# Two-layer decoder: one transposing transfer per causal query tile, weight loads in mid unit, fourth tile finished in its own slot

## The reference

```
# layer 0                                   # layer 1
q, k = rope(x @ Wq), rope(x @ Wk)           q, k = x @ W_Q, x @ W_K      # no rope
v = x @ Wv                                  v = x @ W_V
s = q @ k.T / sqrt(128); s[causal] = -inf   the same
y = softmax(s) @ v ; y @ Wo                 the same
x = layernorm(x + y)
```

## Time and profile before

| | |
|---|---|
| runs of the kernel before | 2684.7 us median, 2680.32 to 2685.36 |
| profiled execution, whole | 2686.01 us |
| its span | 2684.1 us, granted TensorE clock 0.964 on average |
| PE busy | 2436.8 us, 91% of the span |
| DVE, ACT | 1852.3 us (69%), 1587.0 us (59%) |
| POOL | 715.6 us (27%) |

### The profile page before, as it was taken

One profiled execution on the slowest core, in us unless ns is written; L12 is line 12 of the kernel. 1 busy time (PEld: TensorE's weight loads), 2 busy tenths in 40 slices (PEclk: granted clock), 3 DMA queues, 4 the chain that ended last, 5 costly groups with the idle time before them and its releaser, 6 DMA issues. The chain is left out here.

```text
span 2684.1 us, 58413 instructions
## 1 busy us (share of the span) xinstructions
PE 2436.8 (91%) x21345; PEld 1575.8 (59%) x21584; DVE 1852.3 (69%) x3371; ACT 1587.0 (59%) x2718; POOL 715.6 (27%) x671
## 2 busy tenths in 40 slices
PE   6988997989999999999678999998899999999964
PEld 4555664546666666665355666665466666665432
DVE  4776676657777777775556666667478888885597
ACT  4767665158877778874134555554167777774243
POOL 5565656601111011112233222215300000012211
PEclk8999999999999999999888999999899999999987
DMA  3333335325666666666240334435167777776400
GB/s 91 87 75 84 85 73 106 118 48 108 114 116 116 109 111 116 114 112 131 106 165 3 97 86 90 92 84 136 36 123 144 145 145 145 148 150 131 108 0 32
DMA packets 777604, 273.63 MB, mean 102 GB/s; under 512 B 746097, under 2 KB 748913, under 8 KB 775793
## 3 DMA queue, kind: packets, MB, share of 16 engines
q1 hardware_dynamic: 775696, 265.85, 47.0%
q0 software_dynamic: 1760, 5.77, 0.9%
HBM read 84.55 MB, written 6.44 MB: 34 GB/s over the span
## 5 line engine op out<-in xcount | busy, mean ns | idle before, releaser
L846 ACT ACTIVATE ph<-p,ri 128x1024 bf16<-128x1024 f32 (+4 forms) x512 | 437.4, 854 | 455.7 <-DVE ri L1155 367.7
L1165 DVE SCALAR_TENSOR_TENSOR pl<-p,ri,ph 128x1024 bf16<-128x1024 f32 (+4 forms) x512 | 510.5, 997 | 141.0 <-issue 71.7
L1225 PE MATMUL ps<-wo_hi,v_hi 128*128 128x128 bf16 x2688 | 479.2, 220 | 65.8 <-DMA wo_lo<-pl 65.2
L1227 PE MATMUL ps<-wo_hi,v_lo 128*128 128x128 bf16 x2688 | 478.9, 220 | 0.0
L1226 PE MATMUL ps<-wo_lo,v_hi 128*128 128x128 bf16 x2688 | 478.8, 220 | 0.0
L857 ACT ACTIVATE p<-p,nb 128x1024 f32<-128x1024 f32 (+4 forms) x512 | 435.5, 851 | 49.6 <-DVE nb L1148 36.3
L1225 PEld LDWEIGHTS ps<-wo_hi,v_hi 128*128 128x128 bf16 x2688 | 263.6, 98 | 139.4 <-DMA wo_lo<-pl 91.0
L1226 PEld LDWEIGHTS ps<-wo_lo,v_hi 128*128 128x128 bf16 x2688 | 263.9, 98 | 37.4
L1226 PE MATMUL ps<-k_lo,q_hi 128*128 128x512 bf16 (+2 forms) x767 | 271.5, 354 | 7.1 <-issue 0.4
L1227 PE MATMUL ps<-k_hi,q_lo 128*128 128x512 bf16 (+3 forms) x768 | 271.7, 354 | 0.1
L1227 PEld LDWEIGHTS ps<-wo_hi,v_lo 128*128 128x128 bf16 x2688 | 264.1, 98 | 0.0
(11 more groups left out here) (191 smaller groups left out, 5668.9 us busy)
## 6 DMA issues: line engine op xcount, KB each, us to landing
raw_kv<-in_wkvself SPq DMA_DIRECT2D x32, 512.0 KB, 3.6
raw_q<-in_wqself SPq DMA_DIRECT2D x32, 256.0 KB, 2.7
wo_hi<-ph SPq DMA_TRANSPOSE x512, 3.2
wo_lo<-pl SPq DMA_TRANSPOSE x512, 3.1
raw_q<-in_woself SPq DMA_DIRECT2D x32, 256.0 KB, 3.0
raw_q<-in_wqcross SPq DMA_DIRECT2D x32, 256.0 KB, 2.9
raw_q<-in_wocross SPq DMA_DIRECT2D x32, 256.0 KB, 3.0
raw_kv<-in_wkvcross SPq DMA_DIRECT2D x24, 256.0 KB, 3.1
```

What stands on the lines that cost most here:

```text
L846: nc.scalar.activation(m["ph"][:, qt % 2, 0:w], m["p"][:, qt % 2, 0:w], ACT.Copy, scale=ri[:, qt % 2:qt % 2 + 1]).then_inc(p_norm, 1)
L1165: nc.vector.scalar_tensor_tensor(out=m["pl"][:, qt % 2, 0:w], in0=m["p"][:, qt % 2, 0:w], scalar=ri[:, qt % 2:qt % 2 + 1], in1=m["ph"][:, ...
L1225: nc.tensor.matmul(o, l(0), r(0), start=first, stop=False)
L1227: return nc.tensor.matmul(o, l(1), r(0), start=False, stop=last)
```

## The change

1. In causal layers `ph` and `pl` of one tile lie side by side in one tile `phl`, and one transposing transfer moves both, when the remainder is done. SP issues 4 instead of 8 per unit, of 2, 4, 6 and 8 blocks of 128x128. `tr_in` counts 16 for a tile in place of 32 (`landed`).
2. In causal layers the weight loads are issued in the middle of units with n % 4 = 0 and 2, between the transfers of tiles 0 and 1, in place of the start of units 1 and 2.
3. In self0 the split of raw_kv moves from slot 1 to slot 0, that of raw_q from slot 2 to slot 1, and slot 0's rope comes behind the kv split on POOL.
4. In self1 the fourth tile is finished in its own slot on ACT and DVE. Nothing of it is left for the next unit.
5. `units` runs 4 units apart, 6 x 4 in a loop, 4 apart, in all looped stages.

```diff
@@ split_plan
-                first = 1 if self.rope else 2
+                first = 0 if self.rope else 2
@@ units
-            unit(0, None)
-            with engine.Fori(0, 7) as it:
+            for n in range(4):
+                unit(n, None)
+            with engine.Fori(0, 6) as it:
                 for i in range(4):
-                    unit(1 + i, it)
-            for n in range(UNITS - 3, UNITS):
+                    unit(4 + i, it)
+            for n in range(UNITS - 4, UNITS):
                 unit(n, None)
@@ SP, transposed and unit
+                    if L.causal:
+                        sp.wait_ge(p_lo, at(count, n, it))
+                        sp.nop(nofuse=True)
+                        sp.dma_start_transpose(m["pT"][qt][:, 0:2 * w // P, :], m["phl"][:, qt % 2, 0:2 * w]).then_inc(tr_in[qt], 16)
+                        return
...
-                    if n % 4 in (1, 2) and n // 4 < H // 2 - 1:
-                        j = n % 4 - 1
...
+                    loading = n % 4 in ((0, 2) if L.causal else (1, 2)) and n // 4 < H // 2 - 1
...
                             transposed(*((n, it, qt - 1) if qt else (n - 1, it, QT - 1)))
+                        if loading and L.causal and qt == 1:
+                            next_pair()
@@ POOL, unit
-                        if L.rope:
+                        if L.rope and qt:
                             rope(n, it, qt, L.jobs(n, qt))
...
+                        if L.rope and qt == 0:
+                            rope(n, it, qt, L.jobs(n, qt))
@@ ACT, unit
-                        if n or qt:
+                        if qt or n and not (L.causal and not L.rope):
                             rounded(*((n, it, qt - 1) if qt else (n - 1, it, QT - 1)))
...
+                        if (L.causal and not L.rope) and qt == QT - 1:
+                            rounded(n, it, qt)
                         job_parts(n, it, qt, L.jobs(n, qt))
@@ DVE, unit
-                        if n or qt:
+                        pending = qt or n and not (L.causal and not L.rope)
+                        if pending:
                             inverse(*prior)
                         scores(n, it, qt)
                         job_parts(n, it, qt, L.jobs(n, qt), ("QN",))
-                        if n or qt:
+                        if pending:
                             remainder(*prior)
+                        if (L.causal and not L.rope) and qt == QT - 1:
+                            inverse(n, it, qt)
+                            remainder(n, it, qt)
```

More of the change, by code:

```diff
@@ L217, in build, with landed @@
             c["ln"] += NT
+        def landed(L, n):
+            return c_tr[L.name] + (16 if L.causal else 32) * (n + 1)
+        c_tr = dict(self0=0, cross0=16 * UNITS, self1=48 * UNITS, cross1=64 * UNITS)
         def units(engine, unit, L):
@@ L302, in build @@
                 m["any"] = sb("any", [P, B], F32, s)
-            m["ph"] = sb(f"ph{li}", [P, 2, L.kv], BF16, s)
-            m["pl"] = sb(f"pl{li}", [P, 2, L.kv], BF16, s)
+            both = sb(f"phl{li}", [P, 4, L.kv], BF16, s)
+            if L.causal:
+                m["phl"] = both[:, :, :].rearrange("p (s k) n -> p s (k n)", s=2)
+                m["ph"] = lambda qt, w, q=m["phl"]: q[:, qt % 2, 0:w]
+                m["pl"] = lambda qt, w, q=m["phl"]: q[:, qt % 2, w:2 * w]
+            else:
+                m["ph"] = lambda qt, w, q=both: q[:, qt % 2, 0:w]
+                m["pl"] = lambda qt, w, q=both: q[:, 2 + qt % 2, 0:w]
             m["wo"] = [sb(f"wo{li}_{k}", [P, H, D], BF16, s) for k in hl]
             tail = [t[:, H // 2:, :].rearrange("p h n -> p (h n)") for t in m["wo"]]
-            m["pT"] = [t[:, 0:QT * L.kt * P].rearrange("p (i k q) -> p i k q", i=QT, k=L.kt) for t in tail]
+            if L.causal:
+                pairs = [t[:, 0:QT * L.kt * P].rearrange("p (i k q) -> p i k q", i=2, k=2 * L.kt) for t in tail]
+                m["pT"] = [pairs[i // 2][:, i % 2, :, :] for i in range(QT)]
+            else:
+                m["pT"] = [t[:, 0:QT * L.kt * P].rearrange("p (i k q) -> p i k q", i=QT, k=L.kt) for t in tail]
             if L.causal:
@@ L441, in transposed, with next_pair @@
                         sp.nop(nofuse=True)
+                    if L.causal:
+                        sp.wait_ge(p_lo, at(count, n, it))
+                        sp.nop(nofuse=True)
+                        sp.dma_start_transpose(m["pT"][qt][:, 0:2 * w // P, :], m["phl"][:, qt % 2, 0:2 * w]).then_inc(tr_in[qt], 16)
+                        return
                     sp.wait_ge(p_norm, at(count, n, it))
                     sp.nop(nofuse=True)
[L444 removed]
+                    sp.dma_start_transpose(m["pT"][0][:, qt, 0:w // P, :], m["ph"](qt, w)).then_inc(tr_in[qt], 16)
                     sp.wait_ge(p_lo, at(count, n, it))
                     sp.nop(nofuse=True)
[L447 removed]
+                    sp.dma_start_transpose(m["pT"][1][:, qt, 0:w // P, :], m["pl"](qt, w)).then_inc(tr_in[qt], 16)
                 def unit(n, it):
[L450 to L451 removed]
+                    def next_pair():
+                        j = n % 4 // 2 if L.causal else n % 4 - 1
                         sp.wait_ge(w_split, at(lambda n: base + 2 * (n // 4) + j + 1, n, it))
[L453 to L454 removed]
+                        qkv(at(lambda n: n // 4 + 1, n, it), j, None)
+                    loading = n % 4 in ((0, 2) if L.causal else (1, 2)) and n // 4 < H // 2 - 1
+                    if loading and not L.causal:
+                        next_pair()
                     if n == UNITS - 3:
@@ L843, in rounded @@
                     if bn >= 0:
-                        act.wait_ge(tr_in[bq], at(lambda n: 32 * (c["u"] + behind(n, qt, 2)[0] + 1), n, it))
+                        act.wait_ge(tr_in[bq], at(lambda n: landed(L, behind(n, qt, 2)[0]), n, it))
                     act.wait_ge(r_inv, at(lambda n: c["s"] + QT * n + qt + 1, n, it))
-                    nc.scalar.activation(m["ph"][:, qt % 2, 0:w], m["p"][:, qt % 2, 0:w], ACT.Copy, scale=ri[:, qt % 2:qt % 2 + 1]).then_inc(p_norm, 1)
+                    nc.scalar.activation(m["ph"](qt, w), m["p"][:, qt % 2, 0:w], ACT.Copy, scale=ri[:, qt % 2:qt % 2 + 1]).then_inc(p_norm, 1)
                 def unit(n, it):
                     for qt in range(QT):
-                        if n or qt:
+                        if qt or n and not (L.causal and not L.rope):
                             rounded(*((n, it, qt - 1) if qt else (n - 1, it, QT - 1)))
@@ L879, in _ @@
                 units(act, unit, L)
-                rounded(UNITS - 1, None, QT - 1)
+                if not (L.causal and not L.rope):
+                    rounded(UNITS - 1, None, QT - 1)
                 if L.name in EARLY:
@@ L1161, in remainder @@
                     if bn >= 0:
-                        dve.wait_ge(tr_in[bq], at(lambda n: 32 * (c["u"] + behind(n, qt, 2)[0] + 1), n, it))
+                        dve.wait_ge(tr_in[bq], at(lambda n: landed(L, behind(n, qt, 2)[0]), n, it))
                     dve.wait_ge(p_norm, at(lambda n: c["s"] + QT * n + qt + 1, n, it))
                     dve.nop(nofuse=True)
-                    nc.vector.scalar_tensor_tensor(out=m["pl"][:, qt % 2, 0:w], in0=m["p"][:, qt % 2, 0:w], scalar=ri[:, qt % 2:qt % 2 + 1],
-                                                   in1=m["ph"][:, qt % 2, 0:w], op0=ALU.mult, op1=ALU.subtract).then_inc(p_lo, 1)
+                    nc.vector.scalar_tensor_tensor(out=m["pl"](qt, w), in0=m["p"][:, qt % 2, 0:w], scalar=ri[:, qt % 2:qt % 2 + 1],
+                                                   in1=m["ph"](qt, w), op0=ALU.mult, op1=ALU.subtract).then_inc(p_lo, 1)
                 def unit(n, it):
@@ L1199, in _ @@
                 units(dve, unit, L)
-                inverse(UNITS - 1, None, QT - 1)
-                remainder(UNITS - 1, None, QT - 1)
+                if not (L.causal and not L.rope):
+                    inverse(UNITS - 1, None, QT - 1)
+                    remainder(UNITS - 1, None, QT - 1)
                 quantise_run(EARLY.get(L.name, ()))
```

5 lines of the change are left out of this document (3 added, 2 removed).

## The result

The changed kernel takes 2696.7 us, the median of 5 runs (2692.3 to 2705.2), against 2682.6 for the kernel before in the same comparison. The ratio is 1.0058, 95% interval 1.0036 to 1.0080: 14 us slower, outside the range of 2650 to 2694. The profiled execution is the fastest of the five (2692.3 us, span 2690.4). The one of the kernel before took 2686.0 us, 3.4 above its median here, so the two traces account for 6.3 of the 14 us. The two slowest runs (2703 and 2705 us) show a granted clock of 0.963 where the profiled one shows 0.966.

A forecast was written before the change was run, and what follows sets the result against it. Self0 was taken as bound by a 12.77 us ring of ACT and DVE, self1 and cross1 by PE. Self0 -13, tails -12 and self1 +21 gave -4: 2682 us profiled, 2681 as median, put at 2680, range 2650 to 2694.

The forecast's parts named there:

- Self0: Self0: merged transfer and moved loads take off 9.6 us over the units and 4 at the start, -13 together.
- ring: Self0: a cycle of ACT and DVE steps, 12.77 us per unit, in which PE, DMA and POOL are never last.
- room on PE: Self0: PE needs about 11.2 of 12.77 us, leaving 1.6 us against a slow stretch costing 1.7 us.
- The tails: Ends of self0 and self1: fewer issues and no idle fourth tile, -4.8 and -7, together -12.
- the two waits: Self1 load units: fourth tile waits for tile 1's transfer behind the load, then for POOL's wkv_lo; self1 +21.
- Rival B: Self1: the remainder starts before wkv_lo, self1 gains 3.5 us, 2656 us in all; chance 0.25.
- the 0.2 us: Self1 load units: tile 3's remainder is ready 0.2 us after wkv_lo starts, so it stands still; the +21 turns on this.
- long unit: Self1 unit with a load: v_lo at 14.15 us; with the next unit's 10.9 a pair takes 25.05, 14 pairs +22.
- Rival D: Self1: raw_kv lands at 4.6 us, the longest seen, and self0 keeps its excursions: slower, 2700 us; chance 0.23.

The follow-up runs named there:

- merge alone: Changed kernel with changes 2 to 5 undone, so the kernel before plus one transposing transfer per tile in causal layers: 2659.2 us, ratio 0.9918.
- filler: Changed kernel plus 8 unread 128x512 matmuls on PE in odd units of self1, ahead of the projection waiting for v_lo: 2687.5 us, ratio 1.0018.
- POOL order back: Changed kernel with self0's POOL order as before (kv split in slot 1, q split in slot 2, rope ahead): 2699.3 us, ratio 1.0073.
- loads alone: Kernel before plus only the loads' new place (change 2) and the loop it needs (change 5): 2683.1 us, ratio 1.0002.

## Why the prediction was wrong, point by point

**What bounded the kernel**: right. Self0 is a ring of 12.8 us (12.81 measured), self1 bound by PE at 11.16 (the merge alone shows it in every unit), the cross attentions untouched.

**Self0** (forecast -13): its units gave 367.2 - 358.6 = 8.6 of the 9.6, its start 66.7 - 61.2 = 5.5 where I had 4. The size is right, the reason in part wrong, so the match is in part luck. I gave the room on PE to the merge; the merge alone leaves seven stretches (six before), and the stretches are gone from the profiled executions of all kernels with the loads in mid unit.

**The tails** (forecast -12): from the 29th output of self0 to cross0's first it is 179.8 us before and after, so the -4.8 did not come in this execution (175.5 to 182 in the others). In self1 the same distance, to cross1, fell from 164.0 to 155.4: 8.6 where I had 7.

**Self1, the two waits**: right. Landing at 10.14 us after v_lo (forecast 10.2), tile 1 right behind it, remainder 0.13 us behind wkv_lo (0.2), held to 2.54 us (2.5), v_lo at 14.1 (14.15), a clean pair 24.84 (25.05). Rival B, that the 0.2 us fall the other way, happened in none of the 14 load units, but the order was closer than forecast: in two of them the remainder's record even begins 0.01 to 0.03 us before that of wkv_lo, and it is held all the same. With POOL moved behind the remainder this is 0.75 us again. The other order stands in the kernel before, in self0, where DVE's remainder begins 0.17 us ahead of wkv_lo; it keeps its length, and wkv_lo takes 2.43 us in place of 2.13:

```profile
219.30 0.62 DVE L1165 SCALAR_TENSOR_TENSOR pl<-p,ri,ph 128x384 bf16<-128x384 f32 x1
219.47 2.43 POOL L526 TENSOR_TENSOR wkv_lo<-raw_kv,wkv_hi 128x1024 bf16<-128x1024 f32 x1
```

The rule of the Trainium skill ("SBUF — State Buffer", section "Who interferes with whom") gave the right result: whoever issues first keeps the port to its end. The traces agree in both orders, but for the near ties; the held remainders end 0.55 us after wkv_lo, a little less than their own 0.75.

**The step that failed** is the price of the long unit: "With the next unit's 10.9 a pair takes 25.05 us ... 14 pairs: +22". It took only the chain of DVE and ACT and put the clock of a PE that stands idle at nothing. The runs showed what it costs: in self1 six pieces at 1.2 GHz stand behind PE's longest waits on v_lo in the 28 units, and a seventh in the first load unit, ahead of them. The forecast had +21 for self1. Measured are +26.7 in the 28 units and +2.7 in its start (59.6 to 62.3 us from ffn0's last output to self1's first), where the first load unit lies: +29.4. The filler gives back 9.8 and 1.4 of this. The chain of DVE and ACT was sized well: the forecast's 13 x 25.05 = 325.7 us for the pairs with a load compare with 323.4 under the filler and 331.7 without it. The rows of the kernel before had shown the clock for self0: the earlier trace rows price a piece at half clock at 1.4 us, and I used them only for what would go. How firm the 2.7 us are is another matter: that distance is 57.6 to 62.0 us in the other kernels.

**The sum.** Measured in the spans: -14.0 up to cross0, +2.7 + 26.7 - 8.6 in self1, -0.5 elsewhere: +6.3. Forecast -4. Of the 10 us between them 8.4 are self1 with its start and 3.4 the tails, less about 1.5 of small gains. The profiled execution of the filler kernel, 2681.9 us, meets the forecast's 2682, but that is luck: self1 with its start costs 18.1 us there where the forecast had 21, and its tail gives 4.1 where the forecast had 7. The medians differ by 8 us more than the profiled executions. About half of that is the kernel before, whose profiled execution lay 3.4 us above its median. For the other half, the slower runs of the changed kernel have a clock lower by up to 0.003; by an estimate from these numbers, that is five more pieces of 3.41 us at 0.50 in 2700 us. That they lie in self1 is inferred from the run with the POOL order back, a like kernel, which has 7 of them in self1's 28 units and takes 358.2 us there; the runs themselves have no trace. The clock need not be all of it: the other runs of the filler kernel lie 3 to 9 us above its profiled one, at a clock of 0.969 to 0.972 against 0.970.

**Rival D** named the right sign and nearly the median (2700) for the wrong reason. raw_kv landed in 3.5 to 4.8 us, median 3.8, and not at the longest time throughout:

```profile
DMA to landing us min/median/max: 3.5/3.8/4.8
```

**What stays open** is why the loads' place clears self0 of stretches. With the POOL order back PE waits up to 2.1 us for wq_lo there and no stretch comes; with the merge alone it waits up to 2.0 us and 7 come. In the kernel before each of self0's six stretches lies at a wait of 1.5 to 2.6 us, but other waits as long have none. So the length of the wait alone does not decide it, and a wait of 2 us may or may not bring a stretch. Nor is it known where the runs of the loads alone lose the time that its profiled execution gains.

## What to carry to other kernels

When a change lets an instruction wait inside a unit, look for what is queued ahead of the transfer it waits for: here moving one load behind that transfer was worth 43 us, and the rest of the change gained 30 us against the kernel before. Price an idle PE by its clock as well as by its slack: each of PE's waits of 2.6 us or more on v_lo in self1 had 3.41 us or more at half clock behind it, on top of what DVE and ACT cost. And before a vector instruction with two SBUF inputs is placed, ask which POOL instruction will start just ahead of it: here that took 2.5 us in place of 0.75.

## What the runs showed of the hardware

- The stretches at 1.2 GHz in self0 and self1 were 3.41 us long, or twice that, and 3.41 us of them cost 1.4 to 1.6 us of time (8.3 to 9.8 us for six in self1; 14.20 against 12.77 us for one in self0). Eight matmuls whose result nothing reads, put where PE stood still, took them away from that stage in the profiled execution and made the kernel 9 us (self1) and 6 us (self0) faster.
- A transposing transfer of four 128x128 blocks, issued 0.5 us behind a 512 KB load, took 4.0 us in the unit shown (2.7 to 4.8, median 3.8, over self1), in a unit without a load 2.4 us (both in the changed kernel).
- Twice the blocks cost no more to issue: 1.2 us on SP's queue for 2 to 8 blocks, as for 1 to 4 before. Only the larger ones land later: 2.3 us for 2 blocks, 2.4 for 4, 2.8 for 6 and 3.1 for 8 (medians of self1), where the single transfers before took 2.4 to 2.5; the forecast had 2.4 for all.
- A 128x512 remainder that began within 0.2 us of POOL's 128x1024 wkv_lo took 2.49 to 2.70 us in all 14 load units of self1, and 0.75 us when POOL began behind it.
